# A four-block kernel's expert stage: weight splits without drains, expert 3's pieces closer together, and an addition behind each result gather

## The reference

```python
xt = x.reshape(T, H)                       # T = 4096 tokens, H = 256
scores = softmax(xt @ Wr)                  # 8 experts
topk_w, topk_idx = top_k(scores, 2)
topk_w = topk_w / (topk_w.sum(-1) + EPS)
g = silu(einsum('th,ehd->etd', xt, Wg)); u = einsum('th,ehd->etd', xt, Wu)
out_all = einsum('etd,edh->eth', g * u, Wd)          # D = 512
out = sum of the two chosen experts' rows, weighted by topk_w
shared = silu(x @ Sg) * (x @ Su) @ Sd
return out + shared
```

## Time and profile before

| what | value |
|---|---|
| median of 3 runs | 1240.55 us (1233.74 to 1241.84) |
| the profiled execution, its own time | 1243.37 us |
| its span (first to last instruction) | 1241.3 us |
| busy: TensorE / weight loads | 1045.4 us (84%) / 906.8 us (73%) |
| busy: VectorE / ScalarE / GpSimd | 793.1 us (64%) / 459.9 us (37%) / 448.3 us (36%) |
| mean granted clock of TensorE | 0.92 of 2.4 GHz |
| chain that ended last: PE / DVE / issue / DVEq / POOL | 47% / 15% / 14% / 10% / 8% |

### The profile page before, as it was taken

How to read it: one execution, slowest core, us unless ns; L and a number is a source line. 1 busy time by engine, 2 the same in 40 slices (tenths; PEclk the granted TensorE clock), 3 DMA queues, 4 the chain that set the end, 5 groups by cost and what they waited for, 6 DMA issues and landing times.

```text
span 1241.3 us, 19142 instructions
## 1 busy us (share of the span) xinstructions
PE 1045.4 (84%) x5944; PEld 906.8 (73%) x5945; DVE 793.1 (64%) x1339; ACT 459.9 (37%) x781; POOL 448.3 (36%) x407
## 2 busy tenths in 40 slices
PE   5699963599999999999899999079999999723995
PEld 4567742589999998999877878068888888611884
DVE  7978898799999986888693434024444444301787
ACT  6635523234444445667412322012222223200345
POOL 3202003145555545222206655647622000574022
PEclk9989985799999999999899999589999999955998
DMA  6100010000000001111605455353231111332022
GB/s 266 41 28 1 17 60 30 0 2 1 0 0 0 1 1 48 76 52 35 204 1 166 135 157 181 111 169 121 102 101 51 51 54 60 98 104 66 34 86 119
DMA packets 41204, 87.80 MB, mean 71 GB/s; under 512 B 5954, under 2 KB 27716, under 8 KB 39748
## 3 DMA queue, kind: packets, MB, share of 16 engines
q0 software_dynamic: 9696, 35.66, 9.3%
q1 hardware_dynamic: 20660, 39.20, 8.7%
q10 hardware_dynamic: 10800, 12.32, 3.3%
HBM read 57.80 MB, written 29.36 MB: 70 GB/s over the span
## 4 chain that ended last, share of the span: by engine, by line
PE 47%; DVE 15%; issue 14%; DVEq 10%; POOL 8%; POOLq 2%; ACT 2%; DMA 1%; ACTq 0%
PE PS L1705 13%; PE PS L1707 12%; PE PS L1706 12%; PE PS L1829 2%; PE PS L2077 2%; DVEq L1197 2%; DVEq L1302 2%; PE PS L1734 1%; POOL even_rows L922 1%; POOL EWs L914 1%; DVEq L1314 1%; DVEq L1210 1%; POOL EWs L917 1%; DVE hx L1209 1%; POOLq L916 1%
## 5 line engine op out<-in xcount | busy, mean ns | idle before, releaser
L1649 DVE TENSOR_TENSOR hb<-PS,gs 128x512 f32<-128x512 f32 x71 | 49.1, 692 | 193.3 <-ACT gs L716 179.6
L1705 PE MATMUL PS<-EWs,xeh 128*128 x284 | 119.4, 420 | 40.3 <-POOL EWs L917 39.1
L716 ACT ACTIVATE gs<-PS 128x512 f32<-128x512 f32 x71 | 42.5, 599 | 201.3 <-PE PS L1707 199.0
L982 POOL DMA_INDIRECT gathered<-expert_outputs,pos x64 | 61.7, 964 | 145.5 <-DMA expert_outputs<-ye 126.1
L1707 PE MATMUL PS<-EWs,xel 128*128 x284 | 112.0, 394 | 0.0
L1706 PE MATMUL PS<-EWs,xeh 128*128 x284 | 111.4, 392 | 0.0
L1705 PE MATMUL PS<-WGh,bxh 128*128 128x352 f32 x256 | 88.3, 345 | 20.1 <-DVE hv L1296 13.7
L1705 PEld LDWEIGHTS PS<-EWs,xeh 128*128 128x128 f32 x284 | 53.6, 189 | 56.3 <-issue 41.0
L1829 PE MATMUL PS<-WD,htf 128*128 128x256 f32 x384 | 88.5, 380 | 1.6 <-ACT htf L511 1.5
L1705 PE MATMUL PS<-EWs,heh 128*128 x284 | 85.7, 302 | 1.5 <-DVE hel L1653 1.5
L1706 PE MATMUL PS<-WGl,bxh 128*128 128x352 f32 x256 | 85.4, 334 | 0.0
(11 more groups left out here) (362 smaller groups left out, 3022.6 us busy)
## 6 DMA issues: line engine op xcount, KB each, us to landing
raw_of<-experts POOLq DMA_DIRECT2D x6, 1536.0 KB
expert_outputs<-ye SPq DMA_DIRECT2D x71, 128.0 KB
xe<-tokens_by_expert ACTq DMA_DIRECT2D x65, 128.0 KB
xraw<-xT SPq DMA_DIRECT2D x8, 512.0 KB, 5.4
X<-x SPq DMA_DIRECT2D x1, 4096.0 KB, 16.8
tokens<-X SPq DMA_DIRECT2D x8, 512.0 KB, 3.1
y<-X SPq DMA_DIRECT2D x8, 512.0 KB, 2.6
raw_of<-experts SPq DMA_DIRECT2D x2, 1536.0 KB, 9.3
```

Source lines behind the costliest of these rows:

```text
L716: act.activation(gs[:, h], PS[:, 2], ACT.Silu).then_inc(e_si, 1)
L982: pool.indirect_dma_start(out=gathered[c][:, j, t], out_offset=None, in_=YS, in_offset=bass.IndirectOffsetOnAxis(ap=pos[:, j, 4 * c + t:4 ...
L1649: dve.tensor_tensor(hb[:, h], PS[:, 3], gs[:, h], ALU.mult).then_inc(e_hb, 1)
L1705: pe.matmul(out_, wh, vh, start=first, stop=False)
```

## The change

GpSimd alone is changed, in three ways; the other engines' instructions stay as they are, in the same order.

1. The low pieces of `split_part` no longer stand behind a drain. Each high piece adds 1 to a new semaphore `high_part`, and its low piece waits for that count.
2. The order of GpSimd's stream in the dispatch is new. A group's store now always stands behind the gathers of the next group. The load of expert 3's weights and the wait for them come one group later, and its 12 pieces stand closer: behind every gather in groups 10 and 11, behind every second one in groups 12 and 13 (before: behind every second one in groups 9 to 14). The load of expert 4's weights now stands behind all gathers, ahead of the last store.
3. Behind each of the 64 gathers of results stands an addition of 28 columns of zeros, each into 28 columns of its own (`pause`, 7 KB per partition, read by nobody).

```diff
+        pause = sb("pause", [P, NT, 2, 28])
...
                 if half == 0:
-                    pool.tensor_tensor(hi, raw, zrow[:, :].unsqueeze(1).to_broadcast([P, 2, D]), ALU.add)
+                    pool.tensor_tensor(hi, raw, zrow[:, :].unsqueeze(1).to_broadcast([P, 2, D]), ALU.add).then_inc(high_part, 1)
                 else:
-                    pool.drain()
+                    pool.wait_ge(high_part, PARTS // 2 * (e - 2) + n // 2 + 1)
                     last_ = pool.tensor_tensor(lo, raw, hi.bitcast(F32), ALU.subtract)
...
-            def gather_tokens(first, end, split=None):
-                part = 0
+            def gather_tokens(first, end, split=None, part=0, every_=2):
                 for g in range(first, end):
                     if g >= STAGES:
                         pool.wait_ge(d_rows, 16 * (g - STAGES + 1))
                     for n, i in enumerate(range(*GROUPS[g])):
                         fetch(stages[g % STAGES][:, n], i, d_stage[g % 2])
-                        if split is not None and n % 2:
+                        if split is not None and n % every_ == every_ - 1:
                             split_part(split, part)
                             part += 1
-                    if g > first:
+                    if g > 0:
                         keep(g - 1)
-                keep(end - 1)
...
             gather_tokens(2, 8, split=2)
+            gather_tokens(8, 9)
             load_expert(3)
-            gather_tokens(8, 9)
+            gather_tokens(9, 10)
             pool.wait_ge(d_raw2, 16 * 2)
-            gather_tokens(9, 15, split=3)
-            gather_tokens(15, 16)
+            gather_tokens(10, 12, split=3, every_=1)
+            gather_tokens(12, 14, split=3, part=8)
+            gather_tokens(14, len(GROUPS))
             load_expert(4)
-            gather_tokens(16, len(GROUPS))
+            keep(len(GROUPS) - 1)
             loaded(4)
...
                         pool.indirect_dma_start(out=gathered[c][:, j, t], out_offset=None, in_=YS,
                                                 in_offset=bass.IndirectOffsetOnAxis(ap=pos[:, j, 4 * c + t:4 * c + t + 1], axis=0)
                                                 ).then_inc(d_gr[c], 16)
+                        pool.tensor_tensor(pause[:, 4 * c + t, j], zrow[:, 0:28], zrow[:, 0:28], ALU.add)
```

More of the change, by code:

```diff
@@ L287, in build @@
         d_raw2 = sem("d_raw_on")
-        xt_kept, d_lx, p_dev = (sem("d_" + n) for n in ("xt_kept", "lx", "p_dev"))
+        xt_kept, d_lx, p_dev, high_part = (sem("d_" + n) for n in ("xt_kept", "lx", "p_dev", "high_part"))
         (ld_c, ld_wq, ld_wc, ld_x, ld_wo, ld_cp, ld_x0, ld_x1, s_out) = (
```

## The result

The changed kernel takes **1159.85 us** (median of 4 runs, 1156.09 to 1164.16) against 1237.47 for the kernel before (4 runs, 1233.74 to 1241.84): ratio 0.9373, 95% interval 0.9321 to 0.9424. The profiled execution took 1158.67 us with a span of 1156.6, so the span fell by 84.7 us; the forecast had taken off 97.8.

A forecast was written before the change was run, and what follows sets the result against it. TensorE was taken to bound the kernel, losing time to late expert weights and a stall beside unbroken gathers. Savings of 40.4 and 57.4 us (61.1 + 1.8 - 5.5), together 97.8, gave 1143 us, range 1134 to 1212.

The forecast's parts named there:

- likeliest case: Whole kernel: TensorE's waits in the dispatch go and the stall is cured, 1143 us, own range 1134 to 1152; chance 0.50.
- Drains and moved stores: Expert stage: TensorE's waits of 2.3 and 36.8 us for low pieces go, plus 1.3 us of lower clock: 40.4 us.
- group of 8.3 us: Dispatch on GpSimd: four gathers, two pieces and a store take 8.3 us without the drain's 2.29, instead of 10.6.
- expert 4's split: Dispatch: ready at 818.2 with its load moved behind the last gathers; TensorE waits 0 to 4 us, taken as 0.
- slower rival: Dispatch: without drains the stall comes there, TensorE crawls some 107 us; 1308 us with the cure missing too; chance 0.06.
- Stall cured: Shared chunks: additions between gathers let TensorE run, chunk 3 starts 61.1 us earlier and itself takes 1.8 us less; chance 0.50.
- The rival that a break brings nothing: Gathers of results: the additions cure nothing, the stall lasts 7.3 us more, 1207 us; chance 0.28.
- instructions arriving too slowly, with a stock of about 13 us: After the experts: TensorE's instructions come too slowly during unbroken gathers, after a stock of about 13 us; inferred from times.
- Roots behind the gathers: Shared chunk 6: first roots stand behind the 56th gather, ScalarE waits 6 us and TensorE behind it: 5.5 us given back.

The follow-up runs named there:

- Experiment 9: Changed kernel without additions, first roots behind the 48th gather and chunk 2's behind the 56th: 1196.26 us against 1237.33 for the kernel before, chip 11.
- 11: Changed kernel with its additions, first roots behind the 48th gather and chunk 2's behind the 56th: 1154.72 us against 1237.33 for the kernel before, chip 11.
- experiment 1: Changed kernel without its 64 additions, all else as changed: 1136.92 us against 1179.85 for the kernel before, chip 12.
- 5: Kernel before, unchanged, run again on chip 2: 1181.05 us against 1182.65, ratio 0.9988.
- 6: Changed kernel, unchanged, run again on chip 2: 1152.01 us against 1182.65 for the kernel before, ratio 0.9741.
- experiment 2: Kernel before with the 64 additions of 28 columns and nothing else of the change: 1189.98 us against 1179.85, chip 12.

## Why the prediction was right, and where it was off

The likeliest case came: dispatch freed, stall cured, faster. 1159.85 us lies inside 1134 to 1212, 17 us above the forecast of 1143 and outside the likeliest case's own range of 1134 to 1152. The working takes off 97.8 us, the trace 84.7; the 13.1 between them are the following, the forecast first and then what was measured. (The other 3.8 us of the 17 are medians against profiled executions: 1145.6 - 1143 in the forecast and 1159.85 - 1158.67 in the result.)

- **Drains and moved stores, 40.4 us: 35.5.** Of these, 2.6 were there before the stage (its first load is that much earlier), so the change brought 32.9. Every step of it holds: group of 8.3 us; expert 3's load, counted 2.6 us later for that, at 724.4 (forecast 725.5); wait for it 2.06 us (2.5); ready at 770.0 (772.0); expert 4's split ends at 814.7 (818.2), and TensorE doesn't wait for it. What was missing is a term: ScalarE and VectorE run late in places of the dispatch ("remote" waits, 23.5 us over both), which costs TensorE idle times of 0.2 to 2.95 us, 8.0 us in all. That it comes of gathers that are denser by the 2.3 us less in each group is a guess; the kernel before has 3.3 us of such waits. On chip 2, which has no stall, the changed kernel has no "remote" wait and four such idle times in the dispatch, 0.20 to 0.60 us and 1.8 us in all, and the stage gives 38.2 us (first tile to last down projection 361.9 against 400.2); on chip 11 the changed kernel's stage takes 370.5 us, like the 369.9 of the first measurement. So this loss, too, is seen only where the stall is. The slower rival (stall comes into the dispatch) did not come: no stretch there has one matmul each 2.80 us, and the whole loss is 8 us and not 107.
- **Stall cured, 61.1 + 1.8 us: 60.5 + 1.8.** The largest term, and given only 0.50, was right. That the additions cure it is now shown (9 against 11); whether by the break or by the gathers' lower rate (1.53 us each against 1.26) is not. The rival that a break brings nothing is out, with its 1207 us. Experiment 9 is what the same working gives without a cure: no additions take off its 7.3 us, 8 gathers fewer ahead of the stop another 10, so 1190, and it measured 1196. The Trainium skill, "Runtime: NRT & Kernel Launch", section on instruction fetch mechanics, had stood for that rival. Its statement on the fetch is not contradicted (no instruction packet was under way in the stall), the conclusion that was drawn from it, that a break changes nothing, is. My own reading, "instructions arriving too slowly, with a stock of about 13 us", fits the delay of 13.8 us, but so does a fixed place in TensorE's code, and no packet was late.
- **Roots behind the gathers, 5.5 us: 12.1.** The mechanism, ScalarE waiting in chunk 6 behind its third SiLU, is as forecast. Its size was off through the gathers' period: (1113.30 - 1029.24) / 55 = 1.53 us and not 1.38. I had built it on 1.26 us from the stretch in which TensorE, VectorE and ScalarE stood still; where they work, gathers without additions take (1090.88 - 1016.43) / 55 = 1.35 us (experiment 1). On chip 2 it is 1.35 without (5) and 1.54 with them (6), so the cure itself slows the gathers by 10 us over 55 of them, where 7 were forecast.
- **Chunk 4, nothing: 1.0 us** of small ScalarE waits.

What no step of the forecast held: its 61 us exist only on some chips. On chip 2 the same edit brings 31 us (on 12 and 15, which have no stall either, it was not measured whole), and its additions cost between 10 (experiment 2) and 15 us (1136.92 against 1152.01, on two chips with the same time of before). There the rivals' argument against the additions, that nothing needs them, is simply true.

## What to carry to other kernels

Ahead of an edit that cures a stall for which no wait, engine or buffer stands, run the kernel before on more than one chip: here it was 57 us in the first measurement and on chip 11, nothing on chips 2, 12 and 15, and the runs of each measurement agreed within 1%. A drain behind DMA issues cost 2.1 to 3.4 us each here, and a semaphore on the one instruction that matters next to nothing (the low piece starts 0.01 us behind its gather). Durations that are read inside a stall are those of idle neighbours; cost the cured kernel with rows from a stretch in which all engines work.

## What the runs showed of the hardware

- One program has two times: 1176 to 1185 us on chips 2, 12 and 15, 1234 to 1242 in the first measurement and on chip 11. Each chip was measured on one occasion, so the chip can't be told from where the program and its tensors were put on it. The difference, where both have a trace (first measurement and chip 2), is one stretch, in which GpSimd issues gathers back to back and TensorE gets a matmul through each 2.80 us, at intervals that are multiples of 0.70 us.
- Where it is, the stall begins 13.8 us behind the first gather and at the same matmul (in both traces), lasts as long as gathers follow each other at 1.25 us, and ends some 5 us after the last one ahead of a pause. A GpSimd instruction of 0.25 us behind each gather keeps it away (1154.72 us against 1196.26); the gap of 0.30 us that is there anyway doesn't.
- Gathers take 1.25 us each beside idle engines, 1.35 beside busy ones, and 1.53 to 1.54 with an addition behind each.
- Why one measurement has the stall and another doesn't, and what TensorE lacks in it, stays open. No instruction packet was moving, and by TensorE's own progress none was due.
